# A three-layer graph network on one core: node rows of three bf16 parts become one f32 row, one product per tile, one-hots in fixed slots

## The reference, cut to what matters

```python
N_NODES, N_EDGES, D = 12500, 200000, 256
def _sage_layer(x, src, dst, inv_deg, W_self, W_neigh, b):
    agg = jax.ops.segment_sum(x[src], dst, num_segments=N_NODES)
    mean = agg * inv_deg[:, None]
    return x @ W_self + mean @ W_neigh + b
deg = jax.ops.segment_sum(jnp.ones_like(src), dst, num_segments=N_NODES)
inv_deg = 1.0 / jnp.maximum(deg, 1.0)
h = relu(_sage_layer(layernorm(x), ...)); h = relu(_sage_layer(h, ...)); h = _sage_layer(h, ...)
x = x + h
# then, on layernorm(x): a router picks nearly half of all nodes; these get
# gelu(z @ w1 + b1) @ w2 + b2, scaled by their router weight; all get z added
```

## Time and profile before

| | us |
|---|---|
| median of three runs | 7058.9 |
| lowest and highest of them | 7055.39 and 7071.32 |
| the profiled execution | 7076.15 |
| its span | 7074.4 |
| of the span, PE busy | 4579.0 |
| POOL busy | 3887.2 |
| DVE busy | 2607.1 |
| ACT busy | 1084.7 |

### The profile page before, as it was taken

The page is one execution under the profiler, slowest core; times in us unless marked ns, Lnnn a source line. Parts: engine busy times, 40 slices in busy tenths (PEclk is TensorE's granted clock), DMA queues, the critical chain, the costliest instruction groups (busy, mean ns, idle before and its releaser), DMA issues.

```text
span 7074.4 us, 108443 instructions
## 1 busy us (share of the span) xinstructions
PE 4579.0 (65%) x20873; PEld 2778.3 (39%) x20874; DVE 2607.1 (37%) x6727; ACT 1084.7 (15%) x2649; POOL 3887.2 (55%) x4094
## 2 busy tenths in 40 slices
PE   1444555555667777646778656665578998788884
PEld 0112222222333344323456222222256776566664
DVE  6123333444423333311222332333333444455556
ACT  5000001111111112100000000000011223223331
POOL 1654544444466666566666666665666664555551
PEclk9666677777777888767888777777689998989997
DMA  7443444444455555446666555554456664444445
GB/s 232 133 116 109 123 121 124 126 126 126 129 143 146 150 151 151 145 135 185 192 197 208 157 151 147 155 156 137 133 181 187 194 197 116 135 139 136 125 129 181
DMA packets 564997, 1065.13 MB, mean 151 GB/s; under 512 B 154587, under 2 KB 361983, under 8 KB 558527
## 3 DMA queue, kind: packets, MB, share of 16 engines
q0 software_dynamic: 261376, 803.21, 39.9%
q10 hardware_dynamic: 196564, 228.51, 9.5%
q1 hardware_dynamic: 106987, 32.54, 2.0%
HBM read 928.09 MB, written 135.83 MB: 150 GB/s over the span
## 4 chain that ended last, share of the span: by engine, by line
issue 35%; PE 29%; DVEq 10%; DVE 7%; another core or an unknown queue 6%; POOL 5%; ACT 4%; DMA 1%; ACTq 1%; SPq 0%; POOLq 0%
PE agg L890 10%; POOL gath L672 5%; PE y L969 3%; PE agg L892 3%; PE lo L892 2%; PE hid L959 2%; PE y L731 2%; DVEq L1347 2%; PE lo L827 2%; DVEq L1240 1%; DVEq L1340 1%; ACT hidT L1795 1%; DVEq L1223 1%; PE hid L756 1%
## 5 line engine op out<-in xcount | busy, mean ns | idle before, releaser
L672 POOL DMA_INDIRECT gath<-table,idx_ring x4084 | 3885.7, 951 | 3052.3 <-issue 1344.3
L890 PE MATMUL agg<-gath,onehot 128*128 x5216 | 2262.5, 459 | 1392.3 <-issue 1036.4
L890 PEld LDWEIGHTS agg<-gath,onehot 128*128 x5216 | 578.4, 111 | 2287.9 <-issue 1999.8
L892 PE MATMUL agg<-gath,onehot 128*128 x3264 | 1000.4, 306 | 146.3 <-issue 141.5
L1230 DVE TENSOR_SCALAR onehot<-iota_row,window_base,dst_f 128x128 f32 x1632 | 481.2, 361 | 1020.6 <-issue 436.4
L892 PE MATMUL lo<-gath,onehot 128*128 x1952 | 664.2, 340 | 87.8 <-issue 83.0
L1223 DVE TENSOR_TENSOR onehot<-count_ps,dst_f 128x512 f32 x408 | 282.0, 691 | 1147.9 <-remote 607.4
L1223 DVE TENSOR_TENSOR onehot<-hid,dst_f 128x512 f32 x488 | 336.8, 691 | 837.2 <-issue 310.6
L969 PE MATMUL y<-w_sb,hidT 128*128 128x256 f32 x1568 | 420.6, 428 | 143.5 <-ACT hidT L1795 121.2
L892 PEld LDWEIGHTS agg<-gath,onehot 128*128 x3264 | 347.6, 107 | 335.4 <-issue 248.4
L959 PE MATMUL hid<-featT,w_gnn 128*128 128x128 f32 x3136 | 411.2, 290 | 53.9 <-issue 53.6
(11 more groups left out here) (193 smaller groups left out, 4169.3 us busy)
## 6 DMA issues: line engine op xcount, KB each, us to landing
gath<-table,idx_ring POOLq DMA_INDIRECT x4084
dense<-counts_dram ACTq DMA_DIRECT2D x50, 1024.0 KB
table<-split ACTq DMA_DIRECT2D x194, 192.0 KB
counts_dram<-dense ACTq DMA_DIRECT2D x16, 1600.0 KB
rows_f<-y ACTq DMA_DIRECT2D x194, 128.0 KB
dense<-rows_f ACTq DMA_DIRECT2D x48, 512.0 KB
table<-gath ACTq DMA_DIRECT2D x24, 768.0 KB, 3.5
xb<-x ACTq DMA_DIRECT2D x97, 128.0 KB
```

What stands on the lines that cost most here:

```text
L672: g.indirect_dma_start(gath[:, j, 0:PARTS * D], None, table[layer][:, :], bass.IndirectOffsetOnAxis(ap=idx_ring[:, h, i:i + 1], axis=0)).t ...
L890: mm(agg[p][:, 0:2 * D], oh, tile_rows[:, :, 0:2 * D], start=False, **flags)
L892: last = mm(low, oh, tile_rows[:, :, 2 * D:2 * D + lo_cols], start=False, **flags)
```

## The change

The table row becomes one f32 row of 256 values (1024 bytes for 1536). The splitting is gone everywhere: both casts and both subtractions of the first table, and L1191, L1196, L1597 and L1604 later. The separate store of f32 rows goes too, since the dense part reads the table itself. There is one f32 product of 128x256 (257 columns in layer 0) per tile, all into `agg`, so the bank `lo`, its opening product and `copy_low` go, and a window ends with one DVE step where there were three (layer 0) or two (layers 1, 2).

One-hots are f32 and lie in fixed places of a buffer of six blocks: looped blocks alternate between places 0 and 1 in a loop of two blocks per turn, an odd first block has place 2 or 3 by the window's parity, the shared block 4 or 5. Only looped blocks still wait for `slots_free` on DVE. Edge counting moves to windows 4 to 35. In layer 2, slots 42 to 95 keep node ids in the bank of the edge counts, `count_ps`, and use one TENSOR_TENSOR per block.

```diff
-                def block_products(b, last_block=False):
+                def block_products(b, slot, last_block=False):
                     base = pe.snap((b % RING_BLOCKS) * GROUP)
-                    pair = pe.snap(((b + w) % RING_BLOCKS) * GROUP)
                     pe.wait_ge(onehot_ready, b + w + pe_base[layer][0])
                     pe.wait_ge(rows_ready, b + pe_base[layer][1])
                     for j in range(GROUP):
-                        oh = onehot[:, bass.ds(pair, GROUP), :][:, j:j + 1, :]
-                        tile_rows = gath[:, bass.ds(base, GROUP), :][:, j:j + 1, :]
+                        tile_rows = gath[:, bass.ds(base, GROUP), :][:, j:j + 1, 0:cols]
                         flags = ends if last_block and j == GROUP - 1 else free
-                        mm(agg[p][:, 0:2 * D], oh, tile_rows[:, :, 0:2 * D], start=False, **flags)
-                        low = agg[p][:, 0:D] if layer else agg_lo[:, 0:lo_cols]
-                        last = mm(low, oh, tile_rows[:, :, 2 * D:2 * D + lo_cols], start=False, **flags)
+                        last = mm(agg[p][:, 0:cols], onehot[:, slot * GROUP + j, :], tile_rows, start=False, **flags)
                     return last
-                for k, (begin, end) in enumerate(sub_spans(pe, first, shared, parts)):
+                spans = pair_spans(pe, first, shared, parts)
+                with pe.If(first < spans[0][0]):
+                    block_products(first, 2 + p).then_inc(slots_free, 1)
+                for k, (begin, end) in enumerate(spans):
...
-                        with pe.Fori(begin, end) as b:
-                            block_products(b).then_inc(slots_free, 1)
-
-                block_products(shared, last_block=True).then_inc(agg_ready, 1)
+                        with pe.Fori(begin, end, 2) as b:
+                            for slot in range(2):
+                                block_products(b + slot, slot).then_inc(slots_free, 1)
+
+                block_products(shared, 4 + p, last_block=True).then_inc(agg_ready, 1)
...
-                    dve.wait_ge(slots_free, b + dve_base[layer])
+                    if looped:
+                        dve.wait_ge(slots_free, b + dve_base[layer])
+                        dve.sem_inc(dve_turn, 1)
```

More of the change, by code:

```diff
@@ L151, in gnn_ffn_program @@
         group_pairs = sb("group_pairs", [1, COUNT_GROUPS // 2 + 1], I32)
-        lo_sb = [sb(f"lo_sb{p}", [P, D + 1]) for p in range(2)]
         skipped = sb("skipped", [1, 2], I32)
@@ L181, in gnn_ffn_program @@
         featT = [sb(f"featT{p}", [P, KD, P]) for p in range(2)]
-        split = [sb(f"split{p}", [P, PARTS, D], BF16) for p in range(2)]
+        spare = sb("spare", [P, BATCH * D])
+        flag, cand = (sb(name, [P, NT])[:] for name in ("flag", "cand"))
         rest = sb("rest", [P, D])
@@ L226, in gnn_ffn_program @@
         dense_ps = [banks and [t[:, h * D:(h + 1) * D] for t in banks for h in range(2)] for banks in dense_banks]
-        window_ids = [None if bank is None else [bank[:, p * P:(p + 1) * P] for p in range(2)]
-                      for bank in (hid[:, 0, :], count_ps[:], None)]
+        window_ids = [[bank[:, p * P:(p + 1) * P] for p in range(2)]
+                      for bank in (hid[:, 0, :], count_ps[:], count_ps[:])]
         yb = [y0[:], hid[:, 0, :]]
@@ L293, in gnn_ffn_program @@
         dense_done = sem("dense_done")
-        y32_stored = [sem(f"y32_stored{p}") for p in range(2)]
         landed = [sem(f"landed{q}") for q in range(RING_BLOCKS)]
@@ L420, in sub_spans, with pair_spans @@
             return list(zip([first] + cuts, cuts + [end]))
+        def pair_spans(eng, first, end, parts):
+            shift = parts.bit_length() - 1
+            cuts = [eng.snap((first * (parts - k) + end * k) >> shift) if k else first for k in range(parts)]
+            cuts = [eng.snap(cut + ((cut + end) & 1)) for cut in cuts]
+            return list(zip(cuts, cuts[1:] + [end]))
         def parity(w, p):
@@ L1099, in slot_phase0 @@
                 normalise4(turn, q)
-                last_part(turn, q)
-                first_rest(turn, q)
             PREP_TURN = 1
@@ L1785, in slot_layer1 @@
                 if exists(w - 3):
-                    split_store(2, w - 3, earlier(half, p, 3), 1 - p, part)
+                    copy_product(2, w - 3, earlier(half, p, 3), 1 - p)
+                    store_rows(2, w - 3, 1 - p, part)
             over_windows(act, 3, LOAD_LOOPS, slot_layer1)
```

229 lines of the change are left out of this document (59 added, 170 removed).

## The result

The changed kernel takes 7170.5 us, median of four runs (7166.5 to 7179.8), against 7063.6 us (7055.4 to 7071.3) for the kernel before on the same chip. The ratio is 1.0153, with a 95% interval of 1.0136 to 1.0171. It is slower by 107 us, and the forecast was 149 us faster.

What follows compares the result with a forecast made beforehand. No engine was full: POOL's gathers waited for PE, and PE for its instruction stream. Terms -30 + 241 - 153 - 93 - 50 - 60 = -145, from 7076 less 17 to the median, gave 6915 us, range 6550 to 7235.

Steps and rivals of the forecast that it cites:

- first stage: Phase 0, before the first gather: dropped ACT casts and DVE subtractions and a smaller store save 30 us.
- f32 product: PE's tile products in all layers: dearer by 0.10 or 0.22 us per tile, +241 us on the path.
- register work: PE's register operations before tile products: 45% less idle "issue", -153 us, between 0 and -567.
- edge counting moved: Edge counting two slots later: counts are needed in layer 1 only, so it costs nothing.
- bytes: Gather queue moves a third less: faster landings shorten POOL's "remote" waits of 418 us, -60 us.
- DVE's one-hots of layer 2: One operation for four per block in slots 42 to 95: -139 us of DVE work, within the -93 term.
- the rest of DVE and ACT: Dropped splitting, adds and copies: the remainder of DVE's -93 us, and ACT's -50 us.
- the prediction's own last sign of being wrong: PE's register operations: the prediction is wrong if they cost the same time in all, whatever their number.
- Rival (a): PE becomes the bound, above all in layer 2, and hides other savings: slower, 7230 us; chance 0.26.
- Rival (c): What DVE and ACT save is cover only: 7057 us, no change; chance 0.12.
- Rival (b): Slow stretches during gathers come from the transfers and shrink with the bytes: -377 for -60, 6597 us; chance 0.16.

Runs made afterwards that it cites:

- e6: Kernel before with one f32 product of 256 columns per tile for its two bf16 products, sums meaningless; 5807.9 against 5721.8 us, ratio 1.0153.
- e14: The kernel of e6 run again, against the kernel before; ratio 1.0156, +89 us.
- e5: The changed kernel itself on a chip without slow register operations, against the kernel before; 5883.6 against 5721.8 us, ratio 1.0285.
- e3: Changed kernel with two bf16 products per tile and bf16 one-hots, middle and low parts left out; 5782.1 us, ratio 1.0100 to the kernel before.
- e7: Kernel before with only fixed one-hot places (still bf16), two blocks per turn and a separate odd first block; 5821.2 against 5721.8 us, ratio 1.0178.
- e13: The kernel of e7 run again, against the kernel before; ratio 1.0174.
- e17: The kernel of e7 on a chip with slow register operations, against the kernel before; 7385.1 against 7170.4 us, ratio 1.0308.
- e8: Kernel before with only the edge counting moved from windows 2 to 33 to windows 4 to 35; 5785.8 against 5721.8 us, ratio 1.0112.
- e1: Changed kernel with edges counted in windows 2 to 33 again; 5788.9 us, ratio 1.0119 to the kernel before.
- e4: Kernel before with table rows of two bf16 parts, third part neither stored nor gathered, same engine work; 5687.2 against 5721.2 us, ratio 0.9942.
- e16: The kernel of e4 run again, against the kernel before; ratio 0.9936, -38 us.
- e2: Changed kernel with all layer 2 one-hots made by four operations per block again, without node ids in PSUM; 5884.0 us.
- e10: Changed kernel with two bf16 products per tile and edges counted in windows 2 to 33 again; 6998.9 against 7069.6 us for the kernel before, ratio 0.9904.
- e11: The kernel of e8 with the splitting of the sources put back to the slot of window 0; 7105.4 against 7069.6 us for the kernel before, ratio 1.0058.
- e9: The kernel before, unchanged, run again for its trace on a chip with slow register operations; 7059.7 us.

## Why the prediction was wrong, step by step

| term | forecast, us | measured, us |
|---|---|---|
| first stage | -30 | -39 (first gather, to 110.2 us) |
| f32 product | +241 | +86, +89 alone (e6, e14), +102 in the change (e5 less e3) |
| register work (fixed places, two blocks a turn) | -153 | +99, +99 (e7, e13), +215 (e17) |
| edge counting moved | 0 | +64 alone (e8), +95 in the change (e5 less e1) |
| bytes | -60 | -34, -38 (e4, e16) |
| DVE's one-hots of layer 2 | part of -93 | 0 (e5 less e2) |
| the rest of DVE and ACT | part of -93, and -50 | about -12, a remainder |
| register work, DVE and ACT together, in the changed kernel | -296 | +4 with slow register operations (from e10), +40 without |

The remainder is from the chips without slow register operations: the change costs 162 us, and 86 + 99 + 64 - 36 - 39 = 174. That these come within 12 us is in part luck, since they were measured in the kernel before, and e7's 99 us hold instruction fetches of a loop that the changed kernel doesn't have. With the prices in the changed kernel, 102 for the product and 95 for the counting, 162 - 102 - 95 + 36 + 39 = 40 us remain for loops, places, DVE and ACT.

**The step that failed first is the register work.** I took 45% of PE's idle "issue" and turned it into saved time by the share that the tile products have in the chain. The idle time fell as forecast (1261 to 671 us), and the slow operations came down to less than half. The time did not follow. On chips with slow register operations the register work, DVE and ACT together came to about +4 us for the forecast -296 (e10). POOL's waits for PE, which had to fall, rose from 1137 to 1290 us. A slower chip costs the changed kernel nearly what it costs the kernel before (1287 and 1342 us). This is close to the prediction's own last sign of being wrong, that the register operations cost the same time in all, whatever their number. And the edit brings two costs of its own that I had not on the list. The coarser loops and fixed places lose 44 to 47 us in layer 2 (e7, e3). And a loop on DVE, which in the counting stage no longer stays fetched, belongs to e7's 99 us and to the counting's 95.

**The second is one sentence**: "A moved step is the edge counting, two slots later ... so that costs nothing here". I asked who needs the result, and not what covers the work. It left windows of 13 and 12 blocks for windows of 5 or fewer, and the splitting of the sources left window 0 with 40 blocks for window 2. This is 64 us in the kernel before and 95 in the changed one. Alone it would not have turned the sign of -145.

With +4 in place of -296 the forecast's sum would have been +155. So the oversized f32 product would have hidden the missing counting. On the chips with slow register operations these two together make the rest of the loss: e10, without both, is 71 us faster than before, and the change 107 us slower, which is some 175 us for a forecast of 241.

**The f32 product was oversized.** 0.44 us per tile was right. The exposure was not: layer 1 goes at POOL's pace on the chips without slow operations (e1 and e4 start the gathers 1600 to 2600 within 1.1 us of each other), so there it costs nothing at all, and in the trace after, the clock granted in layer 1 is 0.85 for 0.78. It is paid in layer 2 and in the counting stage (61 and 38 us, e5 against e3).

**DVE and ACT** were taken at the share of the chain that they have. In layer 2 of the faster chips PE is the bound, and what DVE saves there is nothing.

**Bytes.** The -60 rested on a misreading. The "remote" waits are 567 us and not 418, and they are waits for PE's signal. They are 560 us with a third fewer bytes. That bytes are worth 34 to 38 us on the other kind of chip, which has no such waits, bears out the size of the term and not its reason.

Rival (a) said that PE becomes the bound and gave 7230 us, near the 7170 measured. That is in the main luck. PE does have the larger part of the chain, and POOL's waits for PE rise. But (a) kept the gain from register work in its sum and did not name the counting stage, in which nearly half of the loss lies. Of the 114 us lost in layer 2, e10 with its bf16 products loses 72 already, without more work on PE. Rival (c), that DVE's and ACT's savings are cover, holds where it was tested, for the one-hots of layer 2 (e2). Rival (b) is not borne out: the long operations stayed as long, 1397 ns, though there are fewer:

```profile
L874 PEldq FUSED_REGOPS  x4920: 3/46/1397, 117.0 to 7055.0; - x197
```

What stays open: what makes a chip be of one kind or the other, what in the coarser loops costs layer 2 its time (47 us in e3, 200 in e17), what decides that a loop is fetched anew, and how the 107 us on the first chip divide further, since of single parts only e17 and e11 ran on such chips.

## What to carry to other kernels

Before you cost a moved step at nothing, name what covers it where it stands and what would cover it where it goes. A loop whose body or whose place in the instructions changes can begin to fetch its instructions anew in each turn: look at the packets of the instruction queues on the page, before and after, ahead of anything else. Look at the longest single wait of a row before you say what the row holds. And an idle time is worth what the engine behind it would do with it, so ask for every term who is waiting for that engine in that stage.

## What the runs showed of the hardware

The same kernel takes 5721 to 5730 us on some chips and 7060 to 7170 on others. On the slower ones, register and branch operations of PE and DVE take 0.7 or 1.4 us now and then during gathers (2400 of them over 0.45 us in e9), on the faster ones never over 0.4 us. On the slower ones the signal of PE's finished block also comes over 1 us late in 340 of 895 recorded cases (trace before), on the faster ones within 15 ns (e4, e5, e8, but for the first). A loop on DVE fetched its instructions anew in each turn, 78 packets of 8 KB in 15 turns, with 30 stalls of 1.8 to 7.4 us (e5), and the same loop with six windows written out ahead of it, not four, did not (e1). An f32 product of 128x256 has a time of 0.44 us at full clock when one follows the other, with its weight loads hidden.
